# End of the second edge stage: linear-attention rows scaled inside the last turns, last sums copied one by one, own rows' products shared between VectorE, GpSimd and ScalarE

## What is computed

```python
alpha = leaky_relu(a_src[src] + a_dst[dst], 0.2)        # src, dst: the edges and one loop per node
ex = exp(alpha - segment_max(alpha, dst)[dst])
out = segment_sum(x_lin[src] * (ex / (segment_sum(ex, dst)[dst] + 1e-16)), dst) + bias
...
h = xn + linear_attention(rmsnorm(xn, w_norm1), w_qkv, w_out, b_out)
mix = h + rmsnorm(h, w_norm2)        # rmsnorm: w * (x * rsqrt(mean(x * x) + 1e-6))
...
x = x + out + mix
```

## Time and profile before

| | |
|---|---|
| runs | 2661.57 us median of 3 (2659.99 to 2661.69) |
| profiled execution | 2660.2 us, of which span 2658.5 us |
| VectorE busy over the span | 1939.0 us (73%) |
| GpSimd / TensorE / ScalarE busy | 1669.3 (63%) / 1613.9 (61%) / 1006.1 (38%) us |
| last mark (turn 60) | 2366.90 us from the span's start |
| all sums copied, own differences begin | 2386.95 |
| second half of the blocks averaged | 2410.87 |
| attention rows added | 2427.97 |
| last stage's first transfer | 2428.94 |

### The profile page before, as it was taken

One profiled execution on the slowest core, in us unless ns is written; L12 is line 12 of the kernel. 1 busy time (PEld: TensorE's weight loads), 2 busy tenths in 40 slices (PEclk: granted clock), 3 DMA queues, 4 the chain that ended last, 5 costly groups with the idle time before them and its releaser, 6 DMA issues. The chain is left out here.

```text
span 2658.5 us, 48210 instructions
## 1 busy us (share of the span) xinstructions
PE 1613.9 (61%) x11708; PEld 1207.5 (45%) x11709; DVE 1939.0 (73%) x6206; ACT 1006.1 (38%) x2697; POOL 1669.3 (63%) x1693
## 2 busy tenths in 40 slices
PE   0037677406666676655699928745665556541898
PEld 0014445404444454442599915534554445430677
DVE  8989996318988888887344457678888888878324
ACT  0003332104555555554333315524444444442432
POOL 3777777766777777724677776077777777742100
PEclk9998887757998989967899969967757677665899
DMA  8000000034333333315344441133333333726101
GB/s 241 2 6 16 15 15 8 2 106 150 102 104 106 106 105 106 106 37 192 94 105 104 107 122 52 36 104 107 104 106 104 106 104 104 154 62 188 40 10 39
DMA packets 169040, 230.99 MB, mean 87 GB/s; under 512 B 72072, under 2 KB 127060, under 8 KB 168819
## 3 DMA queue, kind: packets, MB, share of 16 engines
q0 software_dynamic: 69328, 139.28, 19.4%
q1 hardware_dynamic: 99616, 90.61, 12.1%
HBM read 190.39 MB, written 39.38 MB: 86 GB/s over the span
## 5 line engine op out<-in xcount | busy, mean ns | idle before, releaser
L2366 POOL DMA_INDIRECT e_rows<-mid_table,rec x488 | 484.6, 993 | 211.1 <-issue 135.3
L986 POOL DMA_INDIRECT e_rows<-mid_table,e_rec x440 | 425.8, 968 | 150.5 <-issue 126.5
L256 POOL DMA_INDIRECT mid_sorted<-p_record,p_row x391 | 410.8, 1051 | 160.7 <-issue 122.1
L256 POOL DMA_INDIRECT mid_sorted<-keep_record,keep_row x231 | 225.3, 976 | 86.0 <-issue 68.6
L1172 PE MATMUL e_ps_A<-e_rows,e_hot 128*125 128x260 f32 x880 | 269.9, 434 | 2.4 <-DVE e_rows L1028 2.3
L1662 DVE TENSOR_SCALAR x_hT<-x_ps_h,keep_b1T 128x128 f32<-128x128 f32 x256 | 72.1, 344 | 160.0 <-PE x_ps_y L1701 139.7
L1157 PE MATMUL e_ps_T<-e_identb,e_hot 128*125 128x128 bf16 x440 | 78.1, 263 | 180.4 <-DVE e_hot L1009 180.4
L2711 PE MATMUL e_ps_mT<-keep_ident,room 128*128 128x128 f32 x488 | 111.4, 404 | 115.3 <-DVE room L2390 115.3
L1172 PEld LDWEIGHTS e_ps_A<-e_rows,e_hot 128*125 128x125 f32 x880 | 165.1, 209 | 21.9 <-DVE e_rows L1028 3.6
L1028 DVE TENSOR_TENSOR e_rows<-e_rows 128x512 f32<-128x512 f32 x220 | 150.6, 685 | 2.0 <-ACT e_rows L1130 1.4
L2633 ACT ACTIVATE room<-room 128x66 f32 x488 | 125.4, 257 | 67.9 <-ACT room L2633 52.4
(11 more groups left out here) (615 smaller groups left out, 4442.1 us busy)
## 6 DMA issues: line engine op xcount, KB each, us to landing
mid_expert_in<-p_zrow SPq DMA_DIRECT2D x1, 8192.0 KB
w<-in_L_ffn_w SPq DMA_DIRECT2D x16, 512.0 KB
x_w<-in_L_ffn_w SPq DMA_DIRECT2D x16, 512.0 KB
x_y<-in_L_ffn_b SPq DMA_DIRECT2D x64, 128.0 KB
x_xs<-mid_expert_in SPq DMA_DIRECT2D x64, 128.0 KB
mid_expert_out<-x_y SPq DMA_DIRECT2D x64, 128.0 KB
f_w_all<-in_L_ffn_W SPq DMA_DIRECT2D x16, 512.0 KB
e_rows<-mid_table,rec POOLq DMA_INDIRECT x488
```

The source lines that it names most:

```text
L256: pool.indirect_dma_start(out=to, out_offset=bass.IndirectOffsetOnAxis(ap=row[:, t:t + 1].bitcast(U32), axis=0), in_=record[:, t, :], in_o ...
L986: pool.indirect_dma_start(out=rows[:, s % RING * 2 + j, :], out_offset=None, in_=k["table"], in_offset=bass.IndirectOffsetOnAxis(ap=rec[:, ...
L2366: pool.indirect_dma_start(out=rows[:, j, q, :], out_offset=None, in_=k["table1"], in_offset=bass.IndirectOffsetOnAxis(ap=rec[:, i * TG + q ...
```

## The change

Four things at the end of `stage_edges1`:

- **Rows in the turns.** ScalarE takes the square root of `ms` in two pieces, columns 0 to 19 behind turn 49 and 20 to 24 behind turn 55 (`root`). VectorE takes their reciprocals in turns 50 and 60 (`unroot`) and scales and adds two rows at the end of each of turns 50 to 60 (`scale_row`), each as one multiplication and one addition with waits; the last three rows follow behind the turns, before the wait for the sums. The old root, reciprocal, row loop and addition are gone. `add_gbias` gets a wait.
- **Last sums singly.** For turns 58 to 60 ScalarE waits for each sum instead of all eight.
- **Own rows shared.** The product of the second half's own rows is GpSimd's, behind its last gather; VectorE waits for it (`s_op`).
- **Averages shared.** Of each half's product by the reciprocal weights ScalarE takes the first 24 blocks (first half) or 10 (second), a block an instruction; VectorE the other 25 or 39. SyncE waits for both.

```diff
--- before.py
+++ after.py
@@ -2197,6 +2197,10 @@
         eps6 = m.sb("eps6", [P, 1])
         rec, rms, gbias = k["rec"], k["rms"], k["gbias"]
         GBIAS_FROM = 2 * TN + 3
+        ROOTED = 20
+        ROOTS_AT = (2 * MIXED * 2 + 1, 2 * TN + 5)
+        SCALED_FROM = ROOTS_AT[0] + 1
+        SHARES = (24, 10)
         rows = m.sb("rows", [P, RING, TG, ROW1])
         nodes = m.sb("nodes", [P, G1_BINS, 2 * H])
         to = m.sb("to", [P, G1_BINS])
@@ -2273,7 +2277,10 @@
         s_keep = m.sem("sums_kept")
         s_end = m.sem("own_differences")
         s_oe = m.sem("own_exponentials")
+        s_op = m.sem("own_products")
+        s_rw = m.sem("reciprocal_weights")
         s_done = m.sem("averaged")
+        s_shared = m.sem("averaged_by_scalar")
         s_out = m.sem("written")
         s_q = m.sem("q_staged")
         s_num = m.sem("mix_numerators")
@@ -2346,6 +2353,7 @@
                 sp.dma_start(ownrow[h * B1:(h + 1) * B1], rows_of[:, :, h * W1:(h + 1) * W1]).then_inc(s_own, 16)
             for n, part in enumerate(PARTS):
                 sp.wait_ge(s_done, n + 1)
+                sp.wait_ge(s_shared, n + 1)
                 for h in range(H):
                     sp.dma_start(out_of[:, part, h * HD:(h + 1) * HD], acc[h * B1:(h + 1) * B1, part, 0:HD]).then_inc(s_out, 16)
             sp.wait_ge(s_out, 16 * H * len(PARTS))
@@ -2367,6 +2375,11 @@
                         out=rows[:, j, q, :], out_offset=None, in_=k["table1"],
                         in_offset=bass.IndirectOffsetOnAxis(ap=rec[:, i * TG + q, 0:1].bitcast(U32), axis=0)
                     ).then_inc(s_rows[j], 16)
+            part = PARTS[1]
+            pool.wait_ge(s_own, 16 * H)
+            pool.wait_ge(s_oe, 1)
+            nc.gpsimd.tensor_tensor(ownrow[:, part, :], ownrow[:, part, :],
+                                    spread(own[:, part].unsqueeze(2), P, part.stop - part.start, W1), ALU.mult).then_inc(s_op, 1)
 
         @block.vector
         def _(dve):
@@ -2536,7 +2549,20 @@
                 if u == 0:
                     dve.wait_ge(s_x, TN)
                 xs = k["x"][:, u * TB:(u + 1) * TB, :]
+                o.settle()
                 o.done(v.tensor_tensor(xs, xs, spread(gbias.unsqueeze(1), NP, TB, D), ALU.add))
+
+            def unroot(n):
+                dve.wait_ge(s_var, n + 1)
+                at = (slice(0, ROOTED), slice(ROOTED, TN))[n]
+                o.done(v.reciprocal(k["ms"][:, at], k["ms"][:, at]))
+                dve.wait_ge(s_x, (ROOTED, TN)[n])
+
+            def scale_row(t):
+                o.settle()
+                o.done(v.scalar_tensor_tensor(normed[:, t, :], normed[:, t, :], k["ms"][:, t:t + 1], n2, ALU.mult, ALU.mult))
+                o.settle()
+                o.done(v.tensor_tensor(k["x"][:, t, :], k["x"][:, t, :], normed[:, t, :], ALU.add))
 
             def odd(t):
                 if a_tile(t - 2):
@@ -2568,6 +2594,11 @@
                 if not over:
                     raise_tops(i, add)
                     mixing(i, j, u, odd, even)
+                    if known(i) and i in (SCALED_FROM, TURNS - 1):
+                        unroot(0 if i == SCALED_FROM else 1)
+                    if known(i) and i >= SCALED_FROM:
+                        for t in range(2 * (i - SCALED_FROM), 2 * (i - SCALED_FROM) + 2):
+                            scale_row(t)
                     if known(i) and GBIAS_FROM <= i < GBIAS_FROM + NB:
                         add_gbias(i - GBIAS_FROM)
                 else:
@@ -2581,6 +2612,9 @@
 
             turns(dve, step, range(2), enter, lambda: o.leave(MIXED - 1))
 
+            for t in range(2 * (TURNS - SCALED_FROM), TN):
+                scale_row(t)
+            o.settle()
             dve.wait_ge(s_keep, G1_N)
             o.done(v.tensor_tensor(zend[:, 0, :], own[:], to[:], ALU.add))
             o.done(v.tensor_tensor(zend[:, 1, :], acc[:, :, W1], to[:], ALU.add))
@@ -2590,30 +2624,24 @@
             v.tensor_tensor(own[:], zend[:, 0, :], zend[:, 1, :], ALU.subtract).then_inc(s_end, 1)
             dve.wait_ge(s_own, 16 * H)
             dve.wait_ge(s_oe, 1)
-            for part in PARTS:
+            for n, part in enumerate(PARTS):
                 own_part, sums = ownrow[:, part, :], acc[:, part, 0:W1]
                 w = acc[:, part, HD:W1]
-                n = part.stop - part.start
-                o.done(v.tensor_tensor(own_part, own_part, spread(own[:, part].unsqueeze(2), P, n, W1), ALU.mult))
-                o.settle()
+                if n == 0:
+                    o.done(v.tensor_tensor(own_part, own_part, spread(own[:, part].unsqueeze(2), P, part.stop - part.start, W1), ALU.mult))
+                    o.settle()
+                else:
+                    dve.wait_ge(s_op, 1)
                 o.done(v.tensor_tensor(sums, sums, own_part, ALU.add))
                 o.settle()
 
                 o.done(v.tensor_scalar(w, w, 1e-16, None, ALU.add))
                 o.settle()
-                o.done(v.reciprocal(w, w))
-                o.settle()
-                v.tensor_tensor(acc[:, part, 0:HD], acc[:, part, 0:HD], spread(w, P, n, HD), ALU.mult).then_inc(s_done, 1)
-
-            rs = k["ms"]
-            dve.wait_ge(s_var, 1)
-            o.done(v.reciprocal(rs, rs))
-            o.settle()
-            dve.wait_ge(s_x, TN)
-            for t in range(TN):
-                o.done(v.scalar_tensor_tensor(normed[:, t, :], normed[:, t, :], rs[:, t:t + 1], n2, ALU.mult, ALU.mult))
-            o.settle()
-            o.done(v.tensor_tensor(k["x"][:], k["x"][:], normed, ALU.add))
+                v.reciprocal(w, w).then_inc(s_rw, 1)
+                mine = slice(part.start + SHARES[n], part.stop)
+                dve.wait_ge(s_rw, n + 1)
+                v.tensor_tensor(acc[:, mine, 0:HD], acc[:, mine, 0:HD], spread(acc[:, mine, HD:W1], P, mine.stop - mine.start, HD),
+                                ALU.mult).then_inc(s_done, 1)
 
         @block.scalar
         def _(act):
@@ -2626,8 +2654,12 @@
                 _, blocks = nc.values_load_multi_w_load_instructions(
                     k["bin1"][0:1, bass.ds(i * TG, TG)], engines=[mybir.EngineType.Activation], min_val=0, max_val=G1_BINS - 1,
                     skip_runtime_bounds_check_because="each is a count of blocks begun, less one")
-                wait_alone(act, s_acc, i * TG + TG)
+                last = known(i) and i >= TURNS - 3
+                if not last:
+                    wait_alone(act, s_acc, i * TG + TG)
                 for q, block_of in enumerate(blocks):
+                    if last:
+                        act.wait_ge(s_acc, i * TG + q + 1)
                     if not (known(i) and i == 0 and q == 0):
                         wait_alone(act, s_keep, i * TG + q)
                     nc.scalar.activation(acc[:, bass.ds(block_of, 1), :].rearrange("p a w -> p (a w)"), state[:, j, q, :],
@@ -2681,6 +2713,13 @@
                     keep_hot(i + 1, (j + 1) % RING)
                     act.wait_ge(s_spr, i + 1)
                     nc.scalar.activation(scale[:, j, :], drop[:], ACT.Exp).then_inc(s_scale, 1)
+                    if known(i) and i in ROOTS_AT:
+                        root(ROOTS_AT.index(i))
+
+            def root(n):
+                act.wait_ge(s_sq, (ROOTED, TN)[n])
+                at = (slice(0, ROOTED), slice(ROOTED, TN))[n]
+                nc.scalar.activation(k["ms"][:, at], k["ms"][:, at], ACT.Sqrt, scale=1.0 / D, bias=eps6[0:NP, :]).then_inc(s_var, 1)
 
             act.wait_ge(s_binT, 1)
             nc.scalar.activation(turned[:], ps_mT[0:G1_BINS, 1, 0:2 * P].rearrange("p (a b) -> p a b", a=2), ACT.Copy).then_inc(s_binTk, 1)
@@ -2690,8 +2729,11 @@
             turns(act, step, range(3))
             act.wait_ge(s_end, 1)
             nc.scalar.activation(own[:], own[:], ACT.Exp).then_inc(s_oe, 1)
-            act.wait_ge(s_sq, TN)
-            nc.scalar.activation(k["ms"], k["ms"], ACT.Sqrt, scale=1.0 / D, bias=eps6[0:NP, :]).then_inc(s_var, 1)
+            for n, part in enumerate(PARTS):
+                act.wait_ge(s_rw, n + 1)
+                for b in range(part.start, part.start + SHARES[n]):
+                    last = nc.scalar.activation(acc[:, b, 0:HD], acc[:, b, 0:HD], ACT.Copy, scale=acc[:, b, HD:W1])
+                last.then_inc(s_shared, 1)
 
         @block.tensor
         def _(pe):
```

## The result

The changed kernel takes 2671.95 us, median of 6 runs (2671.53 to 2673.88), against 2661.11 us of the kernel before beside it (2659.81 to 2663.5): 1.0042 times as long, 95% interval [1.0029, 1.0055], which is 10.8 us slower. The profiled execution took 2671.85 us.

A forecast was written before the change was run, and what follows sets the result against it. It took VectorE and the gather as alternating bounds in the turns, then VectorE alone, with the writes next. Turns and rows +10.0 plus tail +4.9 made +14.9 on 2660.2: 2675.2, as a median 2676.6 us, range 2666.5 to 2681.

The forecast's parts named there:

- The case it forecast: Whole kernel: VectorE bounds the turns and VectorE and GpSimd exclude each other; +11 to +19 us, chance 0.62.
- Turns 51 to 59: Loop turns: 17.5 us of rows less 9.1 us of waiting make the mark of turn 60 8.4 us late.
- the gather stays the bound: Rival, in the turns: the gather bounds them and hides the rows; -8.4, sum +6.5 us; chance 0.05 alone.
- Turn 60: Last turn: two rows and a reciprocal, less 0.51 us of VectorE's waiting for TensorE, add 1.6 us.
- The roots: ScalarE behind turns 49 and 55: two square roots with table loads fit its idle time and cost nothing.
- Last sums singly: ScalarE's copies of turns 58 to 60: 24 extra waits pass while the copy before runs; cost 0.
- the bound of 2.6: Last copies: upper limit for 24 extra waits, 0.11 us each, 2.6 us in all.
- The exclusion: Own rows' products and sums: VectorE and GpSimd exclude each other; GpSimd's 8.5 us puts the first reciprocal at t = 16.3.
- ScalarE's share: First half's average: 24 blocks on ScalarE at 0.256 us each take 6.2 us.
- The writes: Behind the averages: sent at t = 22.6, 21.8 us without a gap, last stage at 45.4 instead of 40.5, +4.9 us.
- 206: Rival, in the writes: two queued halves reach 206 GB/s and take 6 us less; sum +9, chance 0.1.
- the rival without exclusion: Own rows: VectorE and GpSimd run at once, first reciprocal at t = 7.8; -2 to +6 us in all, chance 0.1 alone.

The follow-up runs named there:

- z1: The changed kernel with all 25 attention rows scaled behind the averages again, roots still in the turns: 2662.26 us against 2659.57 for the kernel before, 1.0012.
- x4: The changed kernel with VectorE waiting for GpSimd's product ahead of its own first product, so that GpSimd works alone: 3075.13 us in a single run.

## Why the prediction was right

It said 2676.6 us and slower; the median is 2671.95, in the range. The case it forecast (VectorE bounds the turns, the pair excludes each other) is what happened; sizes were off.

- **Turns 51 to 59**, +8.4 predicted; +8.7 measured from mark 49 on, for the nine turns alone +9.5 against the kernel before and +8.4 against z1. No mark from 54 on waits, nearly as said (that of turn 53 still waits 0.84 us), and a turn of 10.0 and 11.55 us was said to be 10.1 and 11.5. That the gather stays the bound fell with z1: without the rows it is 7.9 less. On the chips with slow turns the rows made no difference that can be told either way, but not by this rival: there VectorE waits for scores, not for gathered rows.
- **Turn 60**, +1.6, measured 1.8 by z1.
- **The roots**, 0: right, the second load ended with 2.5 us of the wait left. The Trainium skill (ScalarE: Activation LUTs, What ACT_TABLE_LOAD costs) counts 2.66 us a switch, by which two switches and the root would be an estimated 5.6 us. The trace disagrees: a load is 1.28 us, the root follows after 0.02, and the three took 2.9 of the 5.4 us between the scale and the next exponential.
- **Last sums singly**, 0: wrong, 1.4. The step that failed is that waits already met are passed while the copy before runs. They aren't: the pitch rises by 0.07 us a copy. It lies within the bound of 2.6, which was worked out from the right rows and then set aside. The other half of the reason, that VectorE's additions are ahead, held.
- **The exclusion** was right and its size wrong. GpSimd's product was costed in proportion to a 256-column addition, 8.5 us; alone it is 5.53. The first reciprocal was due at t = 16.3 and came at 13.06. That the traced product is 8.81 long looks like a hit and is none: 3.3 of it are standing.
- **ScalarE's share**, 0.256 us a block: 5.84 / 24 = 0.243, so an overlap of 0.09 a block, if there is one, is nearly all used up again, by the pointer scale as was guessed or by something else; no run separates the two.
- **The writes**: 21.8 us at the rate of before was right; 150 GB/s back to back, no nearer to 206. They were sent 3.6 us sooner than said, and with them the last stage came at t = 41.3 instead of 45.4. This is the largest miss: +4.9 predicted, +0.8 measured.

On the exclusion the trace of before had a longer pair than the 5 columns of the earlier trace rows, which the prediction passed over:

```profile
2442.53 1.48 DVE L3025 TENSOR_TENSOR keep_x<-keep_x,f_rows 125x1280 f32<-125x1280 f32 x1
```
```profile
2442.76 1.84 POOL L2940 TENSOR_TENSOR f_added<-f_rows 125x256 f32<-125x256 f32 x1 [77.72 <-ACT f_rows L2951]
```

GpSimd's addition began inside VectorE's and ended 0.6 us after it; it took 1.84 us, where most of the others take 0.73. So the evidence against the rival without exclusion was stronger than was said.

That the sum is only 2.2 us off is in part luck: the tail was put 4.1 us too dear, and the turns, turn 60 and the copies 0.3, 0.2 and 1.4 too cheap. The sum was 14.9; with the sizes measured it is 12.7 and with the early start of that execution 11.5, and the medians differ by 10.8. Why mark 49 came early isn't known; marks 49 of six kernels lie between 2248.4 and 2252.9, with nothing changed ahead of them that should move them, so it is taken as the scatter of one execution.

## What to carry over

Work put into a loop is free only up to the waits of each turn by itself: the sum over the turns hides that some have 6 us and some none, and eleven rows in the waits cost 0.5 us where twenty-two, two a turn, cost 9.6. Work that runs beside a long transfer at the end is already hidden, if only the transfer starts first: what pays is to send the first part sooner, in smaller parts, rather than to clear the engine behind it. Sharing two-input work between VectorE and GpSimd took the sum of both times here (12.2 us for 3.48 + 5.53 + 3.48), and each engine's standing showed up as a longer duration of its own instruction.

## What the hardware showed that was not expected

- GpSimd's 128x3185 product, with an operand that repeats over 65 columns, takes 5.53 us alone (x4), 1.7 ns a column, where its 256-column additions take 0.73 us, 2.9 ns a column, in x4 as in the earlier trace rows. What makes the difference no run shows.
- A blocked instruction's span in the trace includes its standing, on both engines (8.68 for 3.48, 8.81 for 5.53 us), and its idle time shows nothing.
- A ScalarE copy with a second wait that is already met follows 0.07 us later: 0.436 instead of 0.365 us over 24 copies.
- The same kernel takes 2660 us on one chip and 3060 to 3086 on others, where VectorE waits for TensorE's scores and TensorE stands 37 to 38 us in 100 ahead of the matmuls of the sums. The granted clock over the span is 0.76 to 0.77 there and 0.81 to 0.82 here; which comes of which isn't shown. The rows in the turns, 9.6 us here, made no difference there that can be told.
